# Attention kernel on one core: maxima and reciprocals turned into rows by VectorE block transposes in place of TensorE transposes and a copy

## What is computed

```
def lora_linear(x, W, A, B): return x @ W + 2.0 * (x @ A @ B)
q = lora_linear(x,   Wq, Aq, Bq)      # (8, 256, 32 heads, 32)
k = lora_linear(ctx, Wk, Ak, Bk)      # (8, 256, 8 heads, 32), each used by 4 query heads
v = lora_linear(ctx, Wv, Av, Bv)
attn = softmax(einsum('bhqd,bhtd->bhqt', q, k) / sqrt(32))
out = x + lora_linear(einsum('bhqt,bhtd->bhqd', attn, v), Wo, Ao, Bo)
```

## Time and profile before

| | |
|---|---|
| time, median of 3 runs | 686.3 us (686.13 to 686.67) |
| profiled execution, first to last instruction (span) | 683.2 us |
| median less span | 3.1 us |
| granted TensorE clock over the span | 1.000 |
| PE busy | 673.3 us, 99% |
| DVE busy | 494.3 us, 72% |
| ACT busy | 473.0 us, 69% |
| POOL busy | 367.3 us, 54% |
| share of the chain that ended last: PE | 92% |

### The profile page before, as it was taken

How to read it: one execution, slowest core, us unless ns; L and a number is a source line. 1 busy time by engine, 2 the same in 40 slices (tenths; PEclk the granted TensorE clock), 3 DMA queues, 4 the chain that set the end, 5 groups by cost and what they waited for, 6 DMA issues and landing times.

```text
span 683.2 us, 14943 instructions
## 1 busy us (share of the span) xinstructions
PE 673.3 (99%) x4350; PEld 540.8 (79%) x4350; DVE 494.3 (72%) x978; ACT 473.0 (69%) x1462; POOL 367.3 (54%) x316
## 2 busy tenths in 40 slices
PE   8999999999999999999999999999899999999998
PEld 6798778878887887788778878887777788888886
DVE  4759987786686678678766866877887898855542
ACT  5658888888888888888888888887779343222220
POOL 3547724842772475277247526733877205876732
PEclk9999999999999999999999999999999999999999
DMA  8957765776677578567757856776787234655331
GB/s 282 335 178 199 223 185 142 202 203 173 160 192 191 151 184 213 163 152 203 190 146 187 213 156 156 195 198 177 196 236 236 94 139 155 215 185 184 125 117 68
DMA packets 103798, 124.69 MB, mean 183 GB/s; under 512 B 9280, under 2 KB 85312, under 8 KB 103760
## 3 DMA queue, kind: packets, MB, share of 16 engines
q1 hardware_dynamic: 103760, 124.23, 63.9%
HBM read 86.18 MB, written 38.01 MB: 182 GB/s over the span
## 4 chain that ended last, share of the span: by engine, by line
PE 92%; DMA 4%; DVE 2%; issue 1%; ACT 1%; SPq 0%; POOL 0%; DVEq 0%; POOLq 0%
PE banks L1471 23%; PE banks L1676 17%; PE banks L1469 12%; PE banks L1489 10%; PE banks L1529 9%; PE banks L1516 8%; PE banks L1540 6%; PE banks L1507 2%; PE banks L1450 2%; PE banks L1436 2%; DMA q_parts<-q_stage 1%; DMA q_stack<-q_parts 1%; PE banks L1437 1%; PE banks L1551 1%; DMA r_rows<-turned_sb 1%
## 5 line engine op out<-in xcount | busy, mean ns | idle before, releaser
L899 ACT ACTIVATE banks<-banks,neg_max 128x256 f32<-128x256 f32 x512 | 229.5, 451 | 23.2 <-DVE neg_max L1130 18.1
L783 POOL TENSOR_TENSOR q_stack<-turned_sb,head_mask 8x512 fp32r<-8x512 f32 x128 | 137.4, 1074 | 192.6 <-DVE turned_sb L1156 187.5
L1130 DVE TENSOR_REDUCE neg_max<-banks 128x2 f32<-128x512 f32 x256 | 175.7, 686 | 83.9 <-PE banks L1489 82.6
L910 ACT ACTIVATE probs_t<-banks 128x512 f32<-128x512 f32 x256 | 154.4, 603 | 58.9 <-PE banks L1516 57.9
L1471 PE MATMUL banks<-x_both,w_hi 128*128 128x512 f32 x448 | 162.9, 396 | 0.0
L1469 PE MATMUL banks<-x_both,w_lo 128*128 128x256 f32 x448 | 118.6, 280 | 0.0
L1489 PE MATMUL banks<-k_stack,q_stack 96*128 96x256 f32 x512 | 110.2, 297 | 0.6 <-DMA q_stack<-q_parts 0.5
L1489 PEld LDWEIGHTS banks<-k_stack,q_stack 96*128 96x128 f32 x512 | 80.4, 189 | 34.5 <-ACT banks L899 13.3
L1516 PE MATMUL banks<-q_stack,k_stack 104*128 104x512 f32 x256 | 106.9, 418 | 0.0
L899 ACT ACTIVATION_READ_ACCUMULATOR banks<-banks,neg_max 128x1 f32 x512 | 106.1, 207 | 0.0
L1469 PEld LDWEIGHTS banks<-x_both,w_lo 128*128 128x128 f32 x448 | 84.7, 189 | 9.3
(11 more groups left out here) (158 smaller groups left out, 1196.4 us busy)
## 6 DMA issues: line engine op xcount, KB each, us to landing
q_stack<-q_parts SPq DMA_DIRECT2D x192, 128.0 KB, 3.5
q_parts<-q_stage SPq DMA_DIRECT2D x64, 256.0 KB, 2.8
raw<-ct SPq DMA_DIRECT2D x32, 256.0 KB, 4.6
raw<-xt SPq DMA_DIRECT2D x32, 256.0 KB, 4.3
scales<-r_rows SPq DMA_DIRECT2D x64, 128.0 KB
context<-ctx_stage SPq DMA_DIRECT2D x64, 128.0 KB, 2.3
stage<-xn SPq DMA_DIRECT2D x16, 512.0 KB, 5.1
w_hi<-context SPq DMA_DIRECT2D x14, 512.0 KB, 7.0
```

The lines of the kernel that those rows point to most:

```text
L783: nc.gpsimd.tensor_tensor(q_stack[rows, u % RING, heads], turned_sb[rows, u % 2].unsqueeze(1).broadcast_to([M_ROWS, 2, S]), head_mask[rows ...
L899: last = nc.scalar.activation(score_bank[c % 2][:, S * h:S * (h + 1)], score_bank[c % 2][:, S * h:S * (h + 1)], ACT.Exp, bias=neg_max[:, u ...
L910: nc.scalar.activation(probs_t[:, u % 2, t, 2 * hp:2 * hp + 2, :].rearrange("p a b -> p (a b)"), st_bank[j % 2], ACT.Exp, scale=-1.0).then ...
L1130: nc.vector.tensor_reduce(out=neg_max[:, u % 2, 2 * c:2 * c + 2], in_=score_bank[c % 2].rearrange("p (h t) -> p h t", h=2), axis=AXIS, op= ...
```

## The change

- `turn_max` moves from PE's list to DVE's list and from `c` = 2 to `c` = 0, right behind `split_max`. It is now four DVE transposes of 32 x 32 blocks: each reads 32 partitions of `max_parts` (2 halves of 32 columns) and writes partitions 96 to 127 of `turned_sb`. PE's two transposes and DVE's `copy_turned` are gone, with the semaphore `max_turned` and the PSUM bank that they used.
- `max_parts` has 32 columns for each half in place of 104: the maxima in columns 0 to 7, the reciprocals in columns 8 to 11. `turned_sb` has 128 partitions; the maxima stay on rows 96 to 103, the reciprocals land on rows 104 to 107, from where `put_rows` stores them.
- SP's list is reordered in the loop and in the last batch: `put_rows` and `spread` stand earlier, `store_ctx` mostly later.

```
-        max_parts = sb("max_parts", [P, 2, KM], F32)
+        max_parts = sb("max_parts", [P, 2, HD], F32)
...
-        turned_sb = sb("turned_sb", [KM, 2, S], F32)
+        turned_sb = sb("turned_sb", [P, 2, S], F32)
...
-            sp.dma_start(r_dram[g % 2], turned_sb[0:GH, (g + 1) % 2]).then_inc(r_stored[g % 2], DMA)
+            sp.dma_start(r_dram[g % 2], turned_sb[KM:KM + GH, (g + 1) % 2]).then_inc(r_stored[g % 2], DMA)
...
             def split_max(b, u):
                 both = neg_max[:, u % 2, :].rearrange("p (a h) -> p a h", a=2)
-                hi, lo = (max_parts[:, :, 3 * HD + GH * i:3 * HD + GH * (i + 1)] for i in range(2))
+                hi, lo = (max_parts[:, :, GH * i:GH * (i + 1)] for i in range(2))
                 dve.wait_ge(max_done, b * SLOTS + (4 * u + 4))
-                need(dve, max_turned, b * NG + u)
...
+                dve.wait_ge(max_split, b * NG + (u + 1))
+
+            def turn_max(b, u):
+
+                need(dve, rsum_done, b * NG + u)
                 need(dve, max_placed, b * (2 * NG) + 2 * (u - 1))
                 need(dve, r_stored[(u + 1) % 2], b * (4 * DMA) + DMA * ((u - 3) // 2 + 1))
-                nc.vector.tensor_copy(turned_sb[:, u % 2, :], turned).then_inc(turned_out, 1)
+                for i in range(P // HD):
+                    rows = turned_sb[3 * HD:P, u % 2].rearrange("p (a m) -> p a m", a=2)
+                    last = nc.vector.transpose(rows[:, :, HD * i:HD * (i + 1)], max_parts[HD * i:HD * (i + 1)])
+                last.then_inc(turned_out, 1)
...
-                if c == TURN and u >= 0 and not (last and u > NG):
-                    copy_turned(b, u)
+                if c == 0 and u >= 0 and not (last and u > NG):
+                    turn_max(b, u)
...
-                for qh in range(2):
-                    last = nc.tensor.transpose(turned[:, P * qh:P * (qh + 1)], max_parts[:, qh, :], ident[:])
-                last.then_inc(max_turned, 1)
...
-                if c == TURN and u >= 0 and not (last and u > NG):
-                    turn_max(b, u, last and u >= NG)
```

More of the change, by code:

```diff
@@ L181, in xattn @@
         ctx_bank = banks[:, 4, 0:S]
-        turned = banks[0:KM, 5, 0:S]
         proj_bank = [banks[:, 6 + i, :] for i in range(2)]
@@ L553, in body @@
                 stack_k(1, b + 1, st0)
+                put_rows(0)
                 load_x(0)
-                put_rows(0)
                 send(pos["q", 4, 0])
+                spread(0)
                 store_ctx(-1)
-                spread(0)
                 stack_q(4, fills + 3, st0 + 4)
+                put_rows(1)
                 load_x(1)
@@ L627, in last_body @@
                 stack_q(4, fills + 3, st0 + 4)
+                put_rows(1)
                 late_loads(6, 7)
-                put_rows(1)
                 send(5)
+                spread(1)
                 store_ctx(0)
-                spread(1)
                 stack_q(5, fills + 3, st0 + 8)
+                put_rows(2)
                 first_loads(0, 1)
-                put_rows(2)
+                spread(2)
                 send(6)
@@ L638, in last_body @@
                 store_ctx(1)
-                spread(2)
                 stack_q(6, fills + 4, st0 + 12)
+                put_rows(3)
                 first_loads(2, 3)
-                put_rows(3)
+                spread(3)
                 send(7)
@@ L657, in last_body @@
                     load_ctx(v, v % 2)
-                put_rows(5)
+                spread(5)
                 store_ctx(4)
-                spread(5)
                 put_rows(6)
+                spread(6)
                 store_ctx(5)
-                spread(6)
                 store_first(0)
```

53 lines of the change are left out of this document (22 added, 31 removed).

## The result

The changed kernel takes 688.8 us (median of 9 runs) against 686.1 us for the kernel before in the same series: a ratio of 1.0043, 95% interval 1.0025 to 1.0061. It is slower by 0.4%, where a gain of 0.6% was predicted. Medians are of all runs; the ratios leave out one run of the nine (805.97 us, granted clock 0.753), one each of the experiments `hybrid_both` (3670 us) and `two64` (703.36 us), and the profiled run of `one`, whose span is above its median. The span of the profiled execution is 687.1 us against 683.2.

A forecast was written before the change was run, and what follows sets the result against it. PE was taken as the bound, busy 673.3 of 683.2 us. Terms: -15.0 (PE) + 4.2 (looped batches) + 3.0 (first) + 4.0 (last) = -3.8 us, a time of 682.5 us; 8-in-10 range 676 to 692.5 us.

The forecast's parts named there:

- PE's term: PE's list loses 65 transpose pairs at 0.23 us each, from 1.77 to 1.54 us between scores: -15.0 us.
- The block's length: DVE's four transposes behind each split: 4 x 0.225 us without overlap plus 0.1 us, 1.0 us.
- the no-overlap case: DVE's four transposes run one after another, 0.22 to 0.27 us each; the forecast itself, chance 0.40.
- break-even: Block length behind the split at which costs reach PE's 15.0 us saving: 1.25 us, or 0.29 us a transpose.
- (a): Looped batches: at one split a batch, DVE's low input part follows without a gap; PE held 0.7 us, +4.2 us in six.
- (b): First batch: DVE has 8.2 us idle in 60; half of 6.6 us taken as lost, +3.0 us.
- (c): Last batch: three folds behind splits wait 1.0 us longer each, +3.0 us, and the rest 1.0: +4.0 us.
- SP's order and the earlier turn: Reordered SP list and turned rows ready two slots earlier cost nothing on PE's path: 0, with -1 to +1 us.
- no change: Rival: PE's saving turns wholly into waits for DVE; 685 to 687.5 us, chance 0.17.
- Overlap: Rival: DVE's transposes overlap, 0.14 us each, 0.56 us behind the split; 675.7 us, chance 0.20.
- POOL does not hold the transposes: Rival claimed POOL holds DVE's transposes behind splits, mean 0.36 us, 1.5 us a block; about 694 us, chance 0.23.

The follow-up runs named there:

- hybrid_both: Changed kernel with group 5's DVE transposes one slot later, and PE's transposes plus the copy in first and last batch; 686.56 us, ratio 1.0009.
- two64: Changed kernel with two DVE transposes of 64 partitions a group for four of 32, and two SP stores in pieces of 128 bytes; 695.04 us.
- one: Changed kernel with one DVE transpose of 128 partitions a group, 8 POOL placing instructions and 4 SP store DMAs; 744.72 us, ratio 1.0863.
- u5_late: Changed kernel with group 5's transposes one slot later, at `c` = 1, in every batch but the last; 685.61 us, ratio 0.9982.
- last_late: Changed kernel with the last batch's transposes of groups 1 to 4 two slots later, its others behind the folds' sums; 687.68 us, ratio 1.0021.
- two_rows: Changed kernel with two 64-partition transposes a group and two SP stores of whole 512-byte rows, order mended in DVE's multiply by scales; 681.88 us, ratio 0.9933.
- sp_old: Changed kernel with SP's list in the order of the kernel before; 689.51 us, ratio 1.0048.
- twice: Changed kernel with each DVE transpose made twice, first into a spare tile; 710.26 us, ratio 1.0346.
- one_u5: Changed kernel with one 128-partition transpose a group, group 5's one slot later in all batches but the last; 746.96 us, ratio 1.0886.
- waits_early: Changed kernel with the waits for POOL's placing and the reciprocals' store moved ahead of the split; 687.73 us, ratio 1.0012.
- pe_kept: Changed kernel with PE's two transposes a group put back, of a constant, without waits and unread; 696.16 us, ratio 1.0142.

## Why the prediction was wrong

- **PE's term, -15.0 us,** was right: 1.53 us in place of 1.77 at `c` = 2, and plain groups at 7.30 us where they were 7.52 to 7.55.
- **The block's length is the term that was mis-sized:** 1.28 us in the loop and 1.12 us outside it, not 1.0. The prediction took 0.225 us a transpose and 0.1 us for all changes between instructions. Each takes 0.24 us and starts 0.251 us behind the one before, which fits the no-overlap case. The gap between the split and the first transpose was not in the sum at all. The forecast's own break-even stood at 1.25 us, and by its slope of 15 us for each microsecond 0.12 to 0.28 us are worth 1.8 to 4.2 us of the 7.3.
- **(a), looped batches: 10.3 us and not 4.2.** The place was right and lost 1.1 us a batch instead of 0.7, 6.6 us in six; 0.28 us of that difference is the longer block. What failed beside the size was "once in each batch": a second place, behind group 5's split, lost 0.56 us a batch, 3.4 us in six, and the start of the first looped batch 0.5 us. The prediction had looked only at the busiest stretch. `u5_late` shows the second place alone.
- **(b), first batch:** 3.1 us, predicted 3.0. That is partly luck. Half of 6.6 us is 3.3 and not 3.0, the one half was a guess, and the loss isn't spread evenly as the sum had it: 2.4 of the 3.1 us lie in groups 0, 5, 6 and 7. No experiment aimed at it.
- **(c), last batch: 5.1 us and not 4.0.** The step that failed is that the block in front of the folds goes to PE in full. The three folds wait 1.38 to 1.40 us, under the 1.5 to 1.8 predicted though the block is longer: their waits grew by 2.2 us and not by 3.0. The rest was put at 1.0 us and came to 2.9, of which a fourth fold's wait of 1.49 us is half. Moved away from the folds, the block cost the same (`last_late`); made shorter by 0.5 us a group, it gave back 2.3 us (`two_rows`). Both fit a DVE whose amount of work counts there; no run separates that from the block's length.
- **SP's order and the earlier turn at 0** held (`sp_old`), and the waits for `scales` in the batches are gone, as predicted.
- **The rivals.** What came is "no change" with its mechanism: PE's saving turned wholly into waits for DVE, by 1.3 us more than the upper end of its time. Overlap did not happen. POOL does not hold the transposes: the longest of 260 took 0.243 us, though 63 began while POOL was at work. The cast shows it instead, as in the earlier trace rows: it took up to 1.09 us, and in the five casts over 0.3 us it ended 0.02 to 0.03 us behind an instruction of POOL. That agrees with the Trainium skill, page "SBUF — State Buffer", section "Who interferes with whom", whose list has the cast and no transposes.

That the block is the cause is shown from both sides. Shortened by 0.5 us (`two_rows`) the eight batches fall by 7.4 us and the span by 8.0, 15 us for each microsecond as the prediction had it; that kernel also changes POOL's placing and splits SP's store in two, a change that nothing shows to save time by itself. Lengthened by 0.55 us (`twice`) the first seven batches grow by 13.7 us, since then plain groups lose too. No experiment aimed at the 0.8 us by which the first scores come later. In the profiles of the experiments they come at 45.1 to 46.0 us, once at 47.4, and three with the same prologue as the changed kernel have them at 45.2, 45.5 and 45.7, so it looks like the scatter of single executions.

## What to carry to other kernels

Work that is moved from the bounding engine to one with idle time must be sized at its start-to-start distance, with the gap ahead of its first instruction, and the idle time must be looked up at every place where it goes: here two of eight groups in each looped batch had too little, and one of them was missed. Where DVE is fuller, in the last batch, moving the block to another slot gained nothing. When an instruction costs the same on 32 and on 128 partitions, cut the number of instructions first, but follow what the new layout asks of the engines behind it: of three such kernels two lost more on POOL and SP than DVE had won. A few bytes' worth of layout in a small store can decide whether SP's list is in time.

## What the runs showed of the hardware

- A DVE transpose of fp32 in blocks of 32 x 32, 64 elements a partition, takes 0.239 us on 32 partitions, 0.241 on 64 (`two_rows`) and 0.244 on 128 (`one_u5`).
- Two of them overlap if they read the same partitions (0.17 us from start to start, `twice`) and not if they read others (0.21 us behind one of 0.20, 0.25 behind one of 0.24). The Trainium skill, page "VectorE: DVE Perf Modes", section "Two Vector instructions with no wait between them", has that rule for DVE instructions in general; these runs show it for transposes.
- In the loop, two further waits in front of an instruction that waits for its neighbour anyway made the gap 0.36 us instead of 0.20 (`waits_early`), and 0.10 us of it came back where they were moved to. Outside the loop the same waits left it at 0.20 us.
- SP's issue of a store of 4 rows took 0.33 us in rows of 512 bytes or of 1 KB (`two_rows`, changed kernel), and 0.65 us in pieces of 128 bytes (`two64`).
- Two PE transposes of 128 x 104 in fp32 cost 0.22 to 0.23 us beside matmuls, where their busy time says 0.54 (`pe_kept` and the earlier trace rows).
